# A transformer layer with ternary feed-forward weights: first two ternary blocks made in the output stage, norms ahead of |w| sums, attention's first loads in the latents' stage

## The reference

```python
def _L0_attn_ref(x, w_dq, g_q, w_uq, w_dkv, g_kv, w_ukrope, w_uv, w_uknope, w_o):
    kv = rmsnorm(x @ w_dkv, g_kv)
    k_nope = (kv @ w_uknope)...; v = (kv @ w_uv)...        # 16 heads of 128
    k_rope = rope(x @ w_ukrope)                            # 64, shared by the heads
    q = rmsnorm(x @ w_dq, g_q) @ w_uq                      # 16 heads of 128 + 64
    scores = (q_nope k_nope^T + rope(q_rope) k_rope^T) / sqrt(192), causal
    return (softmax(scores) @ v) @ w_o

def _quantize(w):
    gamma = jnp.mean(jnp.abs(w))
    return jnp.clip(jnp.round(w / (gamma + EPS)), -1.0, 1.0)

x = x + _L0_attn_ref(_layernorm(x), ...)
# feed-forward on h = _layernorm(x), weights 5632 x 2048, 5632 x 2048, 2048 x 5632
x = x + (sigmoid(h @ _quantize(w1).T) * (h @ _quantize(w2).T)) @ _quantize(w3).T
```

## Time and profile before

| | |
|---|---|
| Runs | 3278.05 (median), 3268.89 and 3707.62 us |
| Profiled execution | 3264.87 us; span of the slowest core 3263.3 us |
| Spans of cores 0 to 7 | 3263.3, 3250.7, 3263.0, 3258.2, 3251.3, 3259.4, 3257.2, 3251.0 us |
| Mean granted clock, cores 0 to 7 | 0.981 to 0.985 |
| Busy on core 0: PE, ACT, DVE, POOL | 93%, 45%, 36%, 11% |
| Blocks on core 0 (from the timeline) | latents to 217, attention to 1159, output to 1418, feed-forward to the end |

### The profile page before, as it was taken

How to read it: one execution, slowest core, us unless ns; L and a number is a source line. 1 busy time by engine, 2 the same in 40 slices (tenths; PEclk the granted TensorE clock), 3 DMA queues, 4 the chain that set the end, 5 groups by cost and what they waited for, 6 DMA issues and landing times.

```text
span 3263.3 us, 47967 instructions; the slowest of 8 cores (3250.7 to 3263.3 us)
## 1 busy us (share of the span) xinstructions
PE 3028.5 (93%) x17170; PEld 1499.0 (46%) x17170; DVE 1179.1 (36%) x2101; ACT 1476.1 (45%) x1968; POOL 349.2 (11%) x745
## 2 busy tenths in 40 slices
PE   3887888888989889979999999999999999999999
PEld 2544455555555444434444444444444444444444
DVE  3635767777777734432222222222100000000010
ACT  3436767777777734566666666555200000000000
POOL 0002322332332300000000000111100000000110
PEclk9998999999999999989999999999999999999999
DMA  9225444454454867777777777888622222222342
GB/s 197 79 59 162 144 132 141 132 144 130 143 152 141 192 214 276 287 257 229 228 229 228 228 226 230 286 288 286 210 78 78 78 76 73 78 78 78 129 134 93
DMA packets 119334, 540.32 MB, mean 166 GB/s; under 512 B 16576, under 2 KB 24768, under 8 KB 91840
## 3 DMA queue, kind: packets, MB, share of 16 engines
q1 hardware_dynamic: 93936, 483.50, 45.3%
q0 software_dynamic: 25168, 53.75, 7.5%
HBM read 446.23 MB, written 102.76 MB: 168 GB/s over the span
## 4 chain that ended last, share of the span: by engine, by line
PE 56%; DMA 0%; ACT 0%; issue 0%; POOL 0%; DVE 0%; DVEq 0%; POOLq 0%; ACTq 0%
PE pf L1271 37%; PE pf L1291 18%; DMA stg<-w_p 0%; POOL y L1177 0%; ACT Bs L1202 0%; ACT wq L1198 0%; ACT L1198 0%; DVE wq L1221 0%; DVE BB L1232 0%; DVEq L1229 0%; DVEq L1220 0%; POOLq L1180 0%; POOLq L1176 0%; ACTq L1194 0%
## 5 line engine op out<-in xcount | busy, mean ns | idle before, releaser
L1271 PE MATMUL pf<-BB,wq 128*128 128x512 bf16 x5632 | 1217.8, 379 | 13.8 <-DVE wq L1221 13.8
L1271 PEld LDWEIGHTS pf<-BB,wq 128*128 128x128 bf16 x5632 | 551.5, 98 | 679.6 <-issue 16.4
L1291 PE MATMUL pf<-wq,h_sb 128*128 128x512 bf16 x2816 | 608.1, 379 | 0.0
L1291 PEld LDWEIGHTS pf<-wq,h_sb 128*128 128x128 bf16 x2816 | 275.5, 98 | 332.2
L1189 ACT ACTIVATE dump<-pf 128x1024 f32<-128x1024 f32 x88 | 90.0, 1023 | 710.0 <-PE pf L1271 710.0
L1221 DVE TENSOR_TENSOR wq<-wq,Bs 128x2048 bf16<-128x2048 bf16 x132 | 161.7, 1225 | 643.2 <-ACT Bs L1202 643.2
L1198 ACT ACTIVATE wq<-stg,tcol 128x2048 bf16<-128x2048 f32 x132 | 263.9, 1999 | 212.5 <-PE pf L1291 120.5
L1215 DVE TENSOR_TENSOR h_sb<-dump,pf 128x1024 bf16<-128x1024 f32 x88 | 107.5, 1221 | 586.3 <-PE pf L1271 586.2
L1202 ACT ACTIVATE Bs<-stg,tcol 128x2048 bf16<-128x2048 f32 x132 | 262.4, 1988 | 0.0
L703 PE MATMUL c_r<-kn,qn 128*128 128x512 bf16 (+3 forms) x640 | 187.4, 359 | 25.4 <-DMA qr<-opr 11.9
L833 DVE COPY PTb<-c_t 128x1024 bf16<-128x1024 bf16 (+7 forms) x256 | 146.9, 574 | 170.9 <-PE c_t L742 168.6
(11 more groups left out here) (150 smaller groups left out, 3003.9 us busy)
## 6 DMA issues: line engine op xcount, KB each, us to landing
stg<-w_p SPq DMA_DIRECT2D x132, 1024.0 KB, 6.9
gba<-w_p SPq DMA_DIRECT2D x130, 768.0 KB, 4.3
w1qT<-wq SPq DMA_DIRECT2D x44, 512.0 KB, 6.3
w2qT<-wq SPq DMA_DIRECT2D x44, 512.0 KB, 6.7
w3qT<-wq SPq DMA_DIRECT2D x44, 512.0 KB, 9.1
wq<-w1qT SPq DMA_DIRECT2D x44, 512.0 KB, 3.2
wq<-w2qT SPq DMA_DIRECT2D x44, 512.0 KB, 3.2
wq<-w3qT SPq DMA_DIRECT2D x44, 512.0 KB, 3.3
```

The source lines that it names most:

```text
L1271: ins = e.matmul(px(m, c)[:, hf * 512:(hf + 1) * 512], w[:, kc * 128:(kc + 1) * 128], BB3[:, kc, t0:t0 + 512], start=(kc == 0), stop=(kc = ...
L1291: ins = e.matmul(pu(tl), h_sb[:, c * FT + tl * 128: c * FT + (tl + 1) * 128], w[:, ci * 512:(ci + 1) * 512], start=(c == 0), stop=(c == HC ...
```

## The change

The diff has four parts.

1. **Latents' weights.** `w_dq`, `w_dkv` and `w_ukr_p` are laid out by the host as 128 rows, so that each partition's part of a load is one contiguous piece: 8 KB of f32 in HBM (4 KB of bf16 on the chip) where there were four pieces of 2 KB (1 KB), and one of 4 KB for `w_ukr_p` where there were sixteen of 256 bytes. Eight loads of 512 pieces become eight of 128; one of 2048 becomes one of 128.
2. **Attention's first loads.** The four first weight pieces and the first rope table get buffers that live through both blocks. POOL issues the four loads in the latents once the first latent tile is transposed, SP issues the table after the last x tile. Attention's block starts without them. Two x tiles of the latents now lie in the memory of `qn` and `gba`.
3. **Output stage.** ACT does the copy, the root and the norm of a tile first and its |w| sums after them. The 34 sums are spread over the first 14 tiles (`beside`: three or two each, in the pattern 3, 2, 3, 2, 3, 2, 2, 3, 2, 3, 2, 3, 2, 2) where they were spread over 16. The third load of a tile waits for the first sum of that tile, which now stands behind the norm.
4. **First ternary blocks.** The reductions, the small matmul and the thresholds move from the stage's end to the boundary between tiles 14 and 15; PE waits there for the reductions. SP loads the first block of w1 and of w2 into `stg[0]` and `stg[1]` during tile 14, behind the last |w| sum; ACT takes their four signs and DVE makes the two additions during tile 15 (the second addition ahead of the last copy). The feed-forward block starts with its loads and signs at block 2. To make room, `stg[0]`, `stg[1]`, `wq[0]`, `wq[1]` and `Bs` lie in `qn`, `gba`, `KR`, `P_s` and the rest of `gba`, which live through the whole program.

```diff
-    wdq_hbm = nc.dram_tensor("w_dq", [D, DQ], F32, kind="ExternalInput")
+    wdq_hbm = nc.dram_tensor("w_dq", [128, KC * DQ], F32, kind="ExternalInput")
...
+    KR = nc.alloc_sbuf_tensor("KR", [128, 2048], BF16)
+    qn = nc.alloc_sbuf_tensor("qn", [128, 2, 2048], BF16)
+    gba = nc.alloc_sbuf_tensor("gba", [128, 2, GW], F32)
+    P_s = nc.alloc_sbuf_tensor("Ps", [128, 2, 1024], BF16)
+    gflat = gba[:, :, :].rearrange("p a b -> p (a b)")
+    stg = [qn[:, :, :].rearrange("p a b -> p (a b)").bitcast(F32), gflat[:, 0:2048]]
+    Bs = gflat[:, 2048:3072].bitcast(BF16)
+    wq = [KR[:, :], P_s[:, :, :].rearrange("p a b -> p (a b)")]
...
+        wup = [sb(n, [128, 4, w], BF16) for n, w in (("wuqr", 256), ("wuqn", 128), ("wukn", 128), ("wuv", 256))]
+        s_up = [sem("s_" + n) for n in ("wqr", "wqn", "wkn", "wv")]
+        tab = sb("tab", [128, 2, 512], F32)
+        s_tab = sem("s_tab")
+        first = list(zip(wup, (wuqr_hbm, wuqn_hbm, wukn_hbm, wuv_hbm), s_up))
...
+                e.dma_start(tab[:, :, :], qtab_hbm.ap()[0, :, :]
+                            .rearrange("p (c j) -> p c j", j=512)).then_inc(s_tab, 16)
...
+                def wload(dst, src, width, c, n, s):
+                    k = KC // n
+                    e.dma_start(dst[:, k * c:k * c + k, :],
+                                src.ap()[:, k * width * c:k * width * (c + 1)]
+                                .rearrange("p (k j) -> p k j", j=width)).then_inc(s, 16)
+
                 for c in range(4):
-                    e.dma_start(wdq[:, 4 * c:4 * c + 4, :],
-                                wdq_hbm.ap()[512 * c:512 * c + 512, :]
-                                .rearrange("(k p) j -> p k j", p=128)).then_inc(s_cq[c], 16)
+                    wload(wdq, wdq_hbm, 512, c, 4, s_cq[c])
                 for c in range(4):
-                    e.dma_start(wdkv[:, 4 * c:4 * c + 4, :],
-                                wdkv_hbm.ap()[512 * c:512 * c + 512, :]
-                                .rearrange("(k p) j -> p k j", p=128)).then_inc(s_ck[c], 16)
-                e.dma_start(wukr[:, :, :],
-                            wukr_hbm.ap().rearrange("(k p) j -> p k j", p=128)).then_inc(s_cr, 16)
+                    wload(wdkv, wdkv_hbm, 512, c, 4, s_ck[c])
+                wload(wukr, wukr_hbm, 64, 0, 1, s_cr)
+                e.wait_ge(s_tl, 2)
+                for dst, src, s in first:
+                    e.dma_start(dst[:, :, :], src.ap()[0, :, :].rearrange("p (k j) -> p k j", k=4)
+                                ).then_inc(s, 16)
...
                 for n in range(5):
-                    table(n)
+                    if n > 0:
+                        table(n)
                     if n < GPRE:
                         gload(n)
...
-                wload("rope", 0)
-                wload("qn", 0)
-                wload("kn", 0)
-                wload("v", 0)
...
+    gw = [stg[1], stg[0]]
+
+    def beside(ti):
+
+        return range(min(NW, -(-NW * ti // (NT - 2))), min(NW, -(-NW * (ti + 1) // (NT - 2))))
...
-                j = 0
                 for ti in range(NT):
-                    while j < min(NW, (NW * (ti + 1) + NT - 1) // NT):
+                    for j in beside(ti):
                         gload(j)
-                        j += 1
+                    if ti == NT - 2:
+                        e.wait_ge(s_gu, NW)
+                        for i in range(2):
+                            e.dma_start(stg[i], w_hbm[i].ap()[0:128, :]).then_inc(s_ld[i], 16)
                     e.wait_ge(s_ad, 4 * ti + 4)
                     s_w.i(e.dma_start(xnew_hbm.ap()[ti * 128:(ti + 1) * 128, :], xs[ti % 3]), ti)
...
+                    if ti == NT - 2:
+                        e.wait_ge(s_gs, 1)
+                        e.matmul(ps_g[:, 0:3], ones_f[:, :], gsum[:, :], start=True, stop=True).then_inc(s_gt, 1)
                 trans(NT - 1)
-                e.wait_ge(s_gs, 1)
-                e.matmul(ps_g[:, 0:3], ones_f[:, :], gsum[:, :], start=True, stop=True).then_inc(s_gt, 1)
 
...
+                def ternary(i):
+                    e.wait_ge(s_sgn, i + 1)
+                    e.tensor_tensor(wq[i], wq[i], Bs, op=OP.add).then_inc(s_wq, 1)
...
+                        if n4 == 2 and ti == NT - 1:
+                            ternary(0)
+                    if ti == NT - 2:
+                        e.wait_ge(s_gu, NW)
+                        for m in range(3):
+                            e.reduce_sum(gsum[:, m:m + 1], gpart[:, GAM_OFFS[m]:GAM_OFFS[m + 1]], axis=AX.X)
+                        e.drain().then_inc(s_gs, 1)
...
-                e.wait_ge(s_gu, NW)
-                for m in range(3):
-                    ins = e.reduce_sum(gsum[:, m:m + 1], gpart[:, GAM_OFFS[m]:GAM_OFFS[m + 1]], axis=AX.X)
-                e.drain().then_inc(s_gs, 1)
+                    if ti == NT - 2:
+                        e.wait_ge(s_gt, 1)
+                        for sg in range(2):
+                            ins = e.tensor_scalar(tcol[:, 3 * sg:3 * sg + 3], ps_g[:, 0:3],
+                                                  (0.5 - sg) / (HD * D), 5e-9 * (1 - 2 * sg),
+                                                  op0=OP.mult, op1=OP.add)
+                        ins.then_inc(s_tc, 1)
+                ternary(1)
                 evac(NT - 1)
-                e.wait_ge(s_gt, 1)
-                for sg in range(2):
-                    e.tensor_scalar(tcol[:, 3 * sg:3 * sg + 3], ps_g[:, 0:3],
-                                    (0.5 - sg) / (HD * D), 5e-9 * (1 - 2 * sg), op0=OP.mult, op1=OP.add)
 
             @blk.scalar
             def _(e):
...
-                j = 0
                 for ti in range(NT):
-                    while j < min(NW, (NW * (ti + 1) + NT - 1) // NT):
-                        gamma(j)
-                        j += 1
-                    if ti > 0:
+                    if ti == NT - 1:
+                        e.wait_ge(s_tc, 1)
+                        for i in range(2):
+                            e.wait_ge(s_ld[i], 16)
+                            e.activation(wq[i], stg[i], AF.Sign, bias=tcol[:, 3 + i:4 + i])
+                            if i >= 1:
+                                e.wait_ge(s_wq, i)
+                            e.activation(Bs, stg[i], AF.Sign, bias=tcol[:, i:i + 1]).then_inc(s_sgn, 1)
+                            if i == 0:
+                                evac(ti - 1)
+                    elif ti > 0:
                         evac(ti - 1)
                     e.wait_ge(s_st, ti + 1)
...
+                    for j in beside(ti):
+                        gamma(j)
...
-                    e.dma_start(stg[i % NSTG][:, :],
-                                w_hbm[m].ap()[b * 128:(b + 1) * 128, :]
-                                ).then_inc(s_ld[i % NSTG], 16)
+                    if i >= 2:
+                        e.dma_start(stg[i % NSTG], w_hbm[m].ap()[b * 128:(b + 1) * 128, :]
+                                    ).then_inc(s_ld[i % NSTG], 16)
...
-                for i in range(NI):
+                for i in range(2, NI):
...
+def _row_tiles(w):
+
+    w = np.asarray(w, np.float32)
+    return np.ascontiguousarray(w.reshape(KC, 128, -1).transpose(1, 0, 2)).reshape(128, -1)
...
-        "w_dq": np.ascontiguousarray(np.asarray(L0_attn_w_dq, np.float32)),
+        "w_dq": _row_tiles(L0_attn_w_dq),
```

92 lines of the change are left out of this document (41 added, 51 removed).

## The result

The changed kernel took 3254.68 us, the median of five runs of 3250.72 to 3629.86; its profiled execution 3253.12. Its ratio to the kernel before is 0.9947, with a 95% interval from 0.9927 to 0.9968: some 17 us less, where 35 had been predicted (3243 against 3278.05). A second set of runs gave 0.9968 (0.9947 to 0.9988). The time lies in the predicted range of 3224 to 3265, and within 2% of before, but the gain is half of what the sum gave.

What follows compares the result with a forecast made beforehand. PE, busy 93% of the span, was taken as the bound, so only its standstill or lower-clock time could be won. Core 0's terms, +5 - 9.6 - 15.7 - 8.0, gave -28.3; 3270.6 - 27 gave 3243 us, range 3224 to 3265.

Steps and rivals of the forecast that it cites:

- The latents (+5): Latents: larger weight pieces slow the x tiles, PE's first product near 69, no wait for `w_dkv`; 5 us later.
- Rival (a): Latents: x is not slowed and weights come earlier, -4 and not +5, about 3234 us; chance 0.23.
- Attention's start (-9.6): Start of attention: with weight piece and table there, PE starts when the blocks change; gain 9.6 us.
- The stage's end (-8.0): End of output stage: feed-forward starts at the block change, 12.9 us earlier, less costs; net gain 8.0 us.
- a table load of 1.3: Between tile 15's last statistics and norm: root and sign might need different tables; cost 0 or 1.28 us, 1.28 taken.
- the stall with its clock: Between tiles 14 and 15: PE restarts 2.8 us late behind the reductions, plus 0.8, half of a possible 1.7 clock loss.
- The 5 us of cover: End of tile 14: DVE's wait for the last |w| sums was taken as covered by 5 us.
- The waits inside the stage (-15.7): Output stage: norms first remove PE's waits at tiles 0 and 8 and their lower clock; gain 15.7 us.
- rival (c): Output stage: a wait stays because the copy stands behind a sum with a late load; 7 us less gain; chance 0.08.
- rival (e): Output stage: x loads queue behind SP's third |w| load in six tiles; slower than before, about 3300 us; chance 0.04.
- level: Whole kernel: 3270.6 us, mean of two undisturbed runs and the profile, was the base from which 27 was taken.
- Attention (0): Attention after its start: no term for its length; the earlier start was to carry through as a whole.

Runs made afterwards that it cites:

- experiment 4: The changed kernel with a third buffer for the |w| pieces, so no load of a tile waits for a sum of the same tile; ratio to before 0.9932.
- experiment 5: The kernel before with each tile's norm ahead of its |w| sums and nothing else, 34 sums still over 16 tiles; ratio to before 0.9969.

## Why the prediction was half right

**The latents (+5)** were right in sum and steps: tile 3 at 44.5, the first product at 69.5, no wait for `w_dkv`, +4.8 on core 0 and +4.3 on the mean; the row layout alone made the kernel before 4.4 us slower. Rival (a), which had 0.23, would have needed the first product near 59.

**Attention's start (-9.6)**: 9.1 us on core 0, 8.3 on the mean, for core 0 had waited longer than the others.

**The stage's end (-8.0)**: the parts were 12.9 less a table load of 1.3, and less 3.6 for the stall with its clock. Measured on the mean 12.2 and 4.9, net -7.3. There was no table load: the root follows the last sign and the first sign follows tile 14's norm without one. The stall is 2.5 us where the last sums are on time and the clock holds (seven cores of experiment 4), so the 2.8 was the right size. It grew to 4.9 for two reasons. The 5 us of cover that the prediction gave the last sums were not there: on four cores DVE waited 0.6 to 1.7 us for them. And the clock, which the prediction counted at half, fell on seven of eight cores.

**The waits inside the stage (-15.7)** are where the argument failed. It failed in this step: "The copy of tile t-1 comes after the third sum, at 17 to 18 us, against 25 where PE needs it. So I cost both at nothing". The copy did come then, 17.4 us after the norm began (1303.48 less 1286.09). But behind the copy on the same engine stand the next tile's root and norm. From one norm to the next a tile has 14.7 us and some 2 of slack; here it was 19.2, and PE waited 2.46 and lost 1.7 of clock. The deadline looked at belonged to the copy, and the one that mattered to the instruction after it. Of the 11.6 us of waits that the eight cores had on the mean before, the norms alone win back all (experiment 5); in the changed kernel 4.3 to 4.5 are lost again in tiles 5 and 8 to 12, and the third buffer removes them. This is rival (c), which had 0.08. It was made worse by a thing that the prediction has nowhere: with 34 sums in 14 tiles the first load of a tile is late too (4.07 us here), and in the kernel where it is not (experiment 5) a late third load costs PE nothing. SP's standing at the third load, which rival (e) was about, also showed: DVE waited for x tiles 45 us in all on core 0; but the root never waited for DVE where PE waited for the norm, so PE did not wait for that.

**The size of the sum.** Core 0 lost 15.7 us to waits in the output stage where the mean core lost 11.6, and the sum was made for core 0 with a sideways look at core 5. Made on the means, the forecast is +5 - 9.6 - 11.6 - 8.0 = -24; the measured terms without attention are 4.3 - 8.3 - 7.1 - 7.3 = -18.4. Another 7.5 of the 35 us were no gain at all but level: 3243 was worked out from 3270.6 and is set here against the median of 3278.05, while in three of the four sets of runs of the study the kernel before came at 3265 to 3268.

**Attention (0)** was in no step: it was put at nothing without a reason. In the first profiled execution it took 7.7 us more and in the second 8.3; over all runs the mean span fell by 14.8 and not by 18.4, so what is left for attention is 3.6 us. That is a remainder between all runs and one profile and not a measurement, and it contains whatever else differs between them. The stand of PE that the change removes had kept the lengths together: the versions with a stand of about 9 us, one of them made on purpose, have the narrow spread, and those without it have not. The mean hardly moves (7.2 us slower for 8.3 of stand, with an error of 1.0 to 1.3). What stays open is why, and why the changed kernel's two profiles have longer attention than all other versions.

So of the 9.4 us by which the means fall short of -24.2, the late |w| loads took 4.5 by the profile, the remainder put down to attention 3.6, the start of attention 1.3 (core 0 was not the mean core) and the stall 1.3 beyond its 3.6, against 0.6 at the end and 0.7 in the latents that came out better.

## What to carry to other kernels

When a wait is cleared by reordering one engine's queue, follow every instruction behind the moved one to its own deadline, not just the first; and when work is squeezed into fewer steps, look at the steps that get one piece more than there are buffers, and at whether the step after them starts late. Sum an eight-core change over the cores' means, and let the slowest core's scatter be a term of its own. A larger transfer piece was no gain here, beside a second queue whose tiles PE waits for: it took the other's share, and 4 to 5 us of the span. Two runs of the version that follows from this (third buffer, earlier reductions, small weight pieces, early first loads) gave 0.9905 and 0.9914 of before, against 0.9947 and 0.9968 for the change as made.
